# Another written-out order for all five engines of a four-layer decoder on one core

## The reference

```python
x = _layernorm(x + L0_attn(x))          # causal self attention, 16 heads of 8, rotary
x = _layernorm(x + L0_xattn(x, ctx))    # cross attention to 154 keys
x = _layernorm(x + L0_ffn(x))           # quantised 128 -> 512, depthwise convolution, SiLU, 512 -> 128
x = _layernorm(x + L1_attn(x))          # attention over the 16 heads inside one token
x = _layernorm(x + L1_xattn(x, ctx))
x = _layernorm(x + L1_ffn(x))           # 16 experts, top 2 with a capacity
x = _layernorm(x + L2_attn(x))          # causal self attention, rotary
x = _layernorm(x + L2_xattn(ctx, x))
x = _layernorm(x + L2_ffn(x))           # gated, 128 -> 512 -> 512 -> 512 -> 128
x = _layernorm(x + L3_attn(x))          # one-head attention with a distance bias
x = _layernorm(x + L3_xattn(x, ctx))
x = _layernorm(x + L3_ffn(x))           # 8 experts, weights from a sigmoid zone
```

## Time and profile before

| what | value |
|---|---|
| median of 3 runs | 1580.04 us (1576.17 to 1593.33) |
| the profiled execution's own time | 1574.37 us |
| its span (first to last instruction) | 1572.7 us |
| granted clock of TensorE, mean | 0.924 |
| instructions | 24308 |

### The profile page before, as it was taken

One profiled execution on the slowest core, in us unless ns is written; L12 is line 12 of the kernel. 1 busy time (PEld: TensorE's weight loads), 2 busy tenths in 40 slices (PEclk: granted clock), 3 DMA queues, 4 the chain that ended last, 5 costly groups with the idle time before them and its releaser, 6 DMA issues.

```text
span 1572.7 us, 24308 instructions
## 1 busy us (share of the span) xinstructions
PE 1301.6 (83%) x8762; PEld 608.0 (39%) x8762; DVE 1094.6 (70%) x2373; ACT 735.9 (47%) x1036; POOL 359.0 (23%) x470
## 2 busy tenths in 40 slices
PE   2577888877564768688688999999999999999997
PEld 1234333332232334344233554543344444444554
DVE  3776678779989788898887668847144634258776
ACT  0036557656333414322437553446745555453652
POOL 0334253102431351503633012022211110020000
PEclk8897999898675979899899999999999999999998
DMA  6632132200020031313213134230312331023011
GB/s 155 155 66 51 41 71 53 51 1 2 1 40 2 21 70 32 69 47 67 64 32 77 42 72 97 79 72 19 80 29 41 82 68 68 2 60 77 27 55 53
DMA packets 50354, 86.26 MB, mean 55 GB/s; under 512 B 13750, under 2 KB 42230, under 8 KB 45942
## 3 DMA queue, kind: packets, MB, share of 16 engines
q1 hardware_dynamic: 50238, 84.71, 23.1%
HBM read 66.95 MB, written 15.60 MB: 52 GB/s over the span
## 4 chain that ended last, share of the span: by engine, by line
PE 58%; DVE 23%; issue 6%; ACT 4%; DMA 3%; SPq 3%; POOL 2%; ACTq 0%; POOLq 0%; DVEq 0%
PE ps L913 8%; PE ps L1067 7%; DVE MX L1282 6%; PE ps L839 5%; PE ps L1033 5%; PE ps L1040 5%; PE ps L1034 4%; PE ps L874 3%; PE ps L748 3%; PE ps L846 3%; PE ps L795 3%; PE ps L962 2%; DVE pack L1423 2%; DVE HEADS L1425 2%; DVE HEADS L1434 1%
## 5 line engine op out<-in xcount | busy, mean ns | idle before, releaser
L1282 DVE TENSOR_REDUCE MX<-ps 128x3 f32<-128x462 f32 (+5 forms) x704 | 411.6, 626 | 172.5 <-PE ps L846 145.3
L1713 ACT ACTIVATE WORK<-ps 128x1024 f32<-128x1024 f32 (+1 forms) x352 | 318.8, 945 | 155.2 <-PE ps L874 111.0
L839 PE MATMUL ps<-KH,QH 48*128 48x154 bf16 (+5 forms) x1536 | 136.2, 262 | 115.2 <-DVE MX L1282 79.3
L913 PE MATMUL ps<-WORK,VA 128*18 128x512 f32 (+3 forms) x1536 | 165.3, 517 | 9.1 <-POOL WORK L1954 5.8
L839 PEld LDWEIGHTS ps<-KH,QH 48*128 48x128 bf16 (+1 forms) x1536 | 60.1, 96 | 253.4 <-DVE MX L1282 159.0
L1968 POOL TENSOR_TENSOR HEADS<-HEADS 128x512 f32<-128x512 f32 x64 | 100.2, 1599 | 243.0 <-ACT HEADS L1782 128.1
L1954 POOL TENSOR_SCALAR_AFFINE_SELECT WORK<-WORK 128x256 f32<-128x256 f32 (+1 forms) x192 | 94.6, 501 | 256.2 <-ACT WORK L1713 255.7
L1807 ACT ACTIVATE SIDE<-ps 128x512 f32<-128x512 f32 x96 | 57.1, 597 | 199.8 <-PE ps L1034 199.7
L874 PE MATMUL ps<-QH,KH 54*128 54x512 bf16 (+3 forms) x768 | 115.7, 339 | 15.3 <-ACT WORK L1713 12.1
L1040 PE MATMUL ps<-SIDE 128*128 128x128 f32 x768 | 107.2, 286 | 13.3 <-ACT VA L1694 7.5
L1040 PEld LDWEIGHTS ps<-SIDE 128*128 128x128 f32 x768 | 98.3, 196 | 45.9 <-issue 27.1
(11 more groups left out here) (285 smaller groups left out, 2141.8 us busy)
## 6 DMA issues: line engine op xcount, KB each, us to landing
SIDE<-in_experts SPq DMA_DIRECT2D x96, 192.0 KB, 2.4
scratch<-HQ SPq DMA_DIRECT2D x48, 192.0 KB, 2.8
QH<-scratch SPq DMA_DIRECT2D x48, 192.0 KB
SIDE<-in_wide SPq DMA_DIRECT2D x8, 1024.0 KB, 6.1
QH<-scratch SPq DMA_DIRECT2D x48, 128.0 KB
scratch<-HK SPq DMA_DIRECT2D x16, 192.0 KB, 2.9
QH<-scratch SPq DMA_DIRECT2D x48, 64.0 KB
KH<-scratch SPq DMA_DIRECT2D x16, 192.0 KB
```

The lines of the kernel that those rows point to most:

```text
L839: mms[b] = pe.matmul(banks[b][:, c * pitch:c * pitch + width], qr[b][:, h, t * 128:t * 128 + 128], kr[b][:, h, 0:width], start=(c == 0), s ...
L913: mm = pe.matmul(ps[32 * j:32 * j + 2 * NV, UB, q0:S], lhsT.rearrange("p a c -> p (a c)"), PB[:, (PAIR_BASE[F] + where[pi]) % NSLOT, b, at ...
L1282: dve.tensor_reduce(MX[:, 32 * b + i0:32 * b + i0 + cnt], src, AX.X, ALU.max, negate=True).then_inc(freed, 1)
L1713: act.activation(PB[:, N % NSLOT, :, lo:hi], wide_banks("pair", F, n)[:, :, lo:hi], ACT.Exp).then_inc(sem("exp_done"), 1)
```

## The change

Only the table `STEPS` is another: the same words with the same number of items of each kind, in another order. The three lists of stages, all instructions' code and all waits stay. The first two lines of the table:

```diff
-project*2 base project*3 pieces send max*2 project max project max*3 project max project max*3 project pieces max*3
-project max*3 project max*2 project max*2 project send max*2 project split max turn pieces project*2 max*3 project
...
+project*2 base project*4 pieces send max*4 project*3 max project pieces max*2 project max*2 project max*3 project
+max*4 project max rest max*5 split send max turn project pieces max*2 pair project pair max pair max pair project max
```

More of the change, by code:

```diff
@@ L263 @@
[L263 to L267, removed]
@@ new lines @@
+value pair*4 max value max pair max*2 value max pair*2 max*2 value max value*2 max pair project max*2 value pair value
+max pair max copy pair value pair*2 max send pair max pair value max split value pair*2 max turn project max pair
+value pair max pair value max value pair out value max pair*2 max value copy max value pair*2 max project pair max*2
+pair*2 out value mix pieces value max*2 pair max value pair max*2 pair wo pair square max pair max pair mean max
+value*2 pair*2 max value*2 send copy max pair value x max pair max pair*2 split value project pair value turn pair
@@ new lines @@
+value out pair max value pair max pair*2 max value*3 max project copy pair project max pair project value max out
+pieces pair max mix value pair*3 wo max pair send pair max value max square value max pair max pair value max pair max
+mean max value pair max*2 value x pair max pair value pair copy max value pair max value max pair*2 max split pair
+value pair*3 turn value max project value max value*2 max value project*2 copy project pieces max pair out pair out
+pair max pair mix pair wo value pair*2 max value pair square max send pair max value max value max pair*2 max value
@@ new lines @@
+pair mean value*2 split pair value pair x pair*2 w0 copy pair*2 turn value*2 max pair value pair out pair*3 max*2 pair
+value pair max pair value pair project value project pair value*2 copy pair max out max value pair mix project max
+value max pair max pair value project max copy pieces pair out pair wo send max split value square value mean max turn
+x value copy max out max mix max wo pair max pair square max project mean pair masks value pair max value pair*2 x
+project q0x max pair value max q0t pair project max pair max pair split h0 project copy pieces send turn h0 value
@@ new lines @@
+pair max value max value copy x max mean out f3 max x pair*2 max project max project s3 max project s3 max value
+project pieces pair max value fk3 value copy split pt3*2 send pt3*2 turn out wo mix pair max pair square pair max
+value max pair*2 max mean wo max square value pair max x mean value max x copy pair wide project max pair*2 project
+max pair value max g2 value*2 max copy g2 split out*2 g2 project g2 wide mix project pieces turn wo hid2*2 square
+hid2*2 mean pair send pair hid2 x hid2*3 pair*2 max wo pair max value max pair*2 max value square pair max value max
@@ L331 @@
+mean x fin
 """.split()
```

116 lines of the change are left out of this document (50 added, 66 removed).

## The result

| | before | after |
|---|---|---|
| median, 17 runs each (least to most) | 1587.15 us (1576.17 to 1593.33) | 1593.58 us (1586.74 to 1599.67) |
| the profiled execution's own time, its span | 1574.37, 1572.7 us | 1590.69, 1589.0 us |
| granted clock, mean | 0.924 | 0.919 |

The ratio is 1.0048, with a 95% interval of 1.0027 to 1.0068: about 0.5% slower, 7.6 us (the two medians by themselves differ by 6.4). The forecast was 9 us faster. The 17 runs of before have a median 7 us above that of the first three, and its profiled execution, at 1574.37 us, was faster than any of the 17.

The account below looks back on a forecast made before the run. Bound stage by stage: VectorE from 340 to 850 us, TensorE after 850, nothing full from 137.6 to 157.5. Terms -9 - 2 - 1 + 3 = -9 laid on the 1580.04 median gave 1571 us; range 1544 to 1597.

Parts of the forecast that it names:

- `rest`, forecast -9: Set-up moved from 137.6 to 157.5 us into front 0's maxima, closing a stretch where no engine is full: -9 us.
- The bound of +3.7: Upper end for moving `rest`: the stretch's loss merely moves, TensorE's part is not covered, nothing is gained later.
- Other rows are exchanged between neighbours; no view speaks for a sign, and I take 0: All remaining order changes, a place or two each: taken as 0, their ends left to the rivals.
- First experts, forecast +3: First expert layer's start: two score blocks back to back on VectorE delay TensorE's second down-projection: +3 us, -0.4 to +7.7.
- Turns, forecast -2: VectorE and GpSimd taking turns, fewer stretched L1423 instructions: -2 us, ends -5.2 and +37.
- Table loads, -1: ScalarE reloads its table 71 times instead of 77, mostly hidden: -1 us, ends -7.7 and 0.
- More is won: VectorE's idle time from 183 to 850 us partly closed, a quarter of 106.5 being 27: 1544 us; chance 0.28.
- The TensorE-bound half opens: TensorE's idle 27.4 us after 850 us doubles: 1598 us; chance 0.08.
- Starved experts: Heads1 of batch 2 beside first experts, 550 to 570 us: both blocks pass through, price 21: 1589 us; chance 0.14.
- It doesn't do what it says: Collisions stay and the wait for `rest` only moves to 75 us: 1580 us, within 4; chance 0.12.
- its sign of 12 us: Sign for starved experts: TensorE waits over 12 us between the first two down-projections, with VectorE idle behind it.

Follow-up runs that it names:

- e5: Order of before up to the end of moe1.0 (about 640 us), the new order from there on: 1.0016 of before (0.9986 to 1.0045), median 1588.16 us.
- e1: Order of before with only the set-up item `rest` moved inside the maxima of front 0: 1.0029 of before (1.0004 to 1.0053).
- e8: e2 with `rest` alone put back to its old place, near 135 us: 1.0052 of before (1.0029 to 1.0074).
- e2: New order up to the end of L0a.2 (about 240 us), then the order of before: 0.9948 of before (0.9921 to 0.9976), median 1575.70 us.
- e17: Whole new order up to the eighth score pair of front 0, then the order of before: 0.9989 of before (0.9961 to 1.0017).
- e7: New order to heads1.0, then before's, with `w0` put back behind two pairs of L0x.1's maxima: 1.0048 of before (1.0023 to 1.0073).
- e13: e2 with 24 matmuls, results never read, added in TensorE's first wait: 0.996 of before (0.9941 to 0.9978).
- e6: Kernel after with the second `hs` block of heads1.2 put back behind moe1.0's second down-projection: 1.0043 of before (1.0019 to 1.0067).
- e11: Kernel before once more, unedited, for a second profile: 1577.11 us in its single run.
- e12: Kernel before with 24 matmuls, results never read, added in TensorE's first wait: 0.9995 of before (0.9969 to 1.0022).
- e9: Kernel before with 36 matmuls, results never read, added in TensorE's first wait: 1.0054 of before (1.0026 to 1.0082).

## Why the prediction was wrong

The differences of the ratios by stretch (head, to heads1.0, to moe1.0, the rest), times 1587, are -8.3, +5.9, +6.2 and +3.8 us, in sum the measured +7.6; the last isn't clear of zero (1.0024 and 1.0048 overlap, `e5` includes 1).

**`rest`, forecast -9.** The size fits the head (-8.3 us), and what the prediction said to look for is there: ScalarE's part at 58.7 to 71.6 us, no hole near 140, 1.00 there, no wait before L1206. But the reason was half right. "In the new place TensorE's part must still be done [...] about 3.7 us" and the projection for which "I count nothing, since VectorE's maxima set that stretch" priced the new place too low. `e1` shows what it costs in the order of before: a wait of 6.43 us before L1206 and 7 to 11 us of VectorE's work in 46.5 to 110 (against `e5` and before), at least as much as the hole gave back. The bound of +3.7 for this ("if the stretch's loss merely moves") is close to `e1`'s 1.0029, which is +4.6 us. That it came out at -8.3 rests on what was priced at nothing, the other rows of the head, so the agreement with -9 is luck. `e8` and `e2` show `rest` at -16 among them; `e17` and `e2` suggest that those behind the turn carry most.

**"Other rows are exchanged between neighbours; no view speaks for a sign, and I take 0": this is the step that failed.** Such rows make the order +5.9 us slower from L0a.2 to heads1.0, a stretch for which the sum had no term, and they decide in the head too. Rows a place or two off shift which engine waits; in 225 to 340 that shows as the same TensorE busy time for fewer matmuls at a lower granted clock. `e7` shows the size that one such row can have: `w0` two pairs of maxima later costs 0.63%, about 10 us, as much as the largest named term of the sum. Which exchange loses the 5.9 us isn't settled: `w0` doesn't, and raising the clock with doubled scores doesn't mend it. `e13` shows about half of the lower clock and of VectorE's loss with no change of order there, so the clock is seen with the loss but isn't shown to be its cause.

**First experts, forecast +3 (ends -0.4 and +7.7).** The part from heads1.0 to moe1.0 costs +6.2 us, and nearly all of it is in that place (56.7 to 63.2 us). The place and the wait of TensorE were right, the size half, and the sum's steps were not. It had VectorE 1.3 us idle for the SiLU. In the kernel after the SiLU was done at 566.39, before VectorE came to its product at 567.19, since the "four short rows (1 us)" took 3.1 us: L1489 0.28, L1492 1.19, L1493 1.41, L1494 0.23; with L1427 at 1.71 instead of 0.49 in the block before. GpSimd's weighting (L1968, 560.83 to 566.80) ran beside them. So TensorE waited 13.93: 9.9 us to the end of the two blocks, for which the sum had 7.7, then the four rows and the product. And `e6` shows that the price isn't bound to the doubled block.

The Trainium skill (SBUF — State Buffer, Who interferes with whom) has VectorE and GpSimd share a pair of ports that one instruction holds exclusively. The trace agrees, and shows the side of it that the sum left out: a short instruction with two SBUF operands is stretched too, L1492 to 1.19 us where it takes 0.22 in `e6`. L1494, which starts at 566.93, behind GpSimd's last product, took 0.23.

**Turns, forecast -2.** L1423 gave back 44.4 - 41.7 = 2.7 us, as forecast (mean 1304 ns, within 1.28 to 1.40 us). But L1427 took 1.5 more, L1492 1.0 (1.9 to 2.9 us in four) and L1493 1.2 (1.3 to 2.5), which the sum never looked at: together 1 us lost. Nearly all of that stands in the one place of the first experts. The collisions moved to other instructions.

**Table loads, -1.** There are 71 as forecast (35 of 1283 ns at L1656). No run isolates them.

**The rivals.** "More is won" fell: VectorE idles 72.5 us in the piece of 340 to 850. "The TensorE-bound half opens": it did by some 5 us (32.2 idle), not by 27. "Starved experts" named the place, at 21 us and with VectorE idle; TensorE's wait passed its sign of 12 us, but VectorE worked through it, and the cost was 6. "It doesn't do what it says" (only the wait for `rest` moves) is what `e1` measured, but not what the change as a whole does. Nearly every local sign named for the forecast came out (TensorE's idle time behind 850 us didn't quite), and the sum was still wrong: they tested the terms, not the remainder at 0.

**The base.** The forecast of 1571 was laid on 1580.04. Against the median of 17 runs it is 1578; 7 of the 22.6 us between 1571 and 1593.58 are the base's.

A version that beats both: `e2`, 0.9948 of before and, by the ratios, 1.0% under after. It takes the new order only up to L0a.2.

## What to carry to other kernels

When a change rewrites a whole order, the remainder "a place or two elsewhere" is not zero with a small error: here it was +5.9 us in one stretch and perhaps +3.8 in another, against a forecast gain of 9, and one word moved behind two pairs of maxima cost about 10. So give it a range of its own, and try the order cut off at stage ends, which shows which part pays. A wait that is moved is to be priced in the new place as fully as in the old one, with the work that stood there; alone, `rest` lost about 5 us, and with the order fitted around it won 16. When collisions between two engines are taken off one instruction, list every other instruction that can be hit.

## What the runs showed of the hardware

The granted clock in the first 110 us varies from run to run with one and the same order: 0.93, 0.86 and 0.60 from 46.5 to 83 us in three profiles (before, `e11`, `e5`), with VectorE's work there at 31.52, 30.46 and 26.15 us. The time lost is not always won back: `e5` was 7.8 us behind at 125 us and 13.5 at 600, `e11` 4.8 behind at 125 and level at 495. The 17 runs of before spread by 17 us, so one profile is a base to about half a per cent only. And TensorE kept busy through its first wait had a full clock there, but 0.67 in the maxima behind it (`e12`; 0.88 in `e9`), no higher than the 0.60 to 0.93 of runs without, and no time was won.
